# Turning routed rows on VectorE from square block loads, with up weights kept on chip, in a two-layer fp32 kernel

## The reference

```
xn = layernorm(x)
s  = attention(xn)            # two query heads, one key/value head, rope, causal softmax
g  = silu(moe(xn))            # 8 experts, top 2 of softmax(router)
x  = x + s * g
xn = layernorm(x)
s  = recurrent(xn)            # conv, decays, cumulative sums, gated feed-forward of width 512
g  = silu(tanh(xn @ w @ a1 @ a2 + bias))
out = x + s * g

moe(x) = sum over e in top2(x) of  p_e(x) * (w2_e @ (gelu(wg_e @ x + bg_e) * (w1_e @ x + b1_e)) + b2_e)
```

## Time and profile before

| | us |
|---|---|
| median of 3 runs | 563.06 |
| the three runs | 563.06, 565.64, 561.0 |
| span of the profiled execution | 567.0 |

### The profile page before, as it was taken

The page is one execution under the profiler, slowest core; times in us unless marked ns, Lnnn a source line. Parts: engine busy times, 40 slices in busy tenths (PEclk is TensorE's granted clock), DMA queues, the critical chain, the costliest instruction groups (busy, mean ns, idle before and its releaser), DMA issues. The chain is left out here.

```text
span 567.0 us, 13345 instructions
## 1 busy us (share of the span) xinstructions
PE 536.0 (95%) x3276; PEld 396.7 (70%) x3277; DVE 385.5 (68%) x1080; ACT 280.6 (50%) x797; POOL 259.1 (46%) x391
## 2 busy tenths in 40 slices
PE   9997999998989999999999999998799999999974
PEld 4745677666759999999999999964444444554441
DVE  6889777886764555555555555559588789778641
ACT  5624565645564555555555554565535644553420
POOL 4305535666502444444444444525356555664210
PEclk9998999999998999999999999999799999999998
DMA  9920553111106788878888788455000000000000
GB/s 285 392 76 33 184 195 94 61 42 61 42 14 180 235 238 233 233 233 234 237 235 237 225 241 228 134 167 144 2 0 19 18 20 0 18 18 1 19 18 18
DMA packets 46107, 71.77 MB, mean 127 GB/s; under 512 B 6256, under 2 KB 32016, under 8 KB 45824
## 3 DMA queue, kind: packets, MB, share of 16 engines
q1 hardware_dynamic: 31536, 57.82, 34.4%
q0 software_dynamic: 4320, 8.92, 4.6%
q10 hardware_dynamic: 10224, 4.73, 3.0%
HBM read 54.14 MB, written 15.74 MB: 123 GB/s over the span
## 5 line engine op out<-in xcount | busy, mean ns | idle before, releaser
L1253 DVE SCALAR_TENSOR_TENSOR AR<-bank,B1T,AR 128x128 f32<-128x128 f32 x284 | 80.0, 344 | 73.0 <-ACT AR L1667 63.1
L523 POOL DMA_INDIRECT rows_y<-YO,DST x71 | 69.8, 982 | 93.2 <-DVE YO L1237 82.5
L1667 ACT ACTIVATE AR<-bank,BGT 128x128 f32<-128x128 f32 x284 | 81.2, 368 | 60.0 <-PE bank L823 53.4
L479 POOL DMA_INDIRECT slots_x<-XR,SLOT x64 | 63.0, 984 | 50.9 <-DMA slots_x<-XR,SLOT 31.0
L823 PE MATMUL bank<-AR,WGE 128*128 128x128 f32 x568 | 75.9, 277 | 0.3 <-ACT AR L1660 0.3
L831 PE MATMUL bank<-AR,WGE 128*128 128x128 f32 x568 | 75.9, 277 | 0.0
L840 PE MATMUL bank<-W2E,AR 128*128 x568 | 75.2, 275 | 0.7 <-DVE AR L1253 0.5
L823 PEld LDWEIGHTS bank<-AR,WGE 128*128 128x128 f32 x568 | 69.8, 193 | 0.6 <-issue 0.6
L831 PEld LDWEIGHTS bank<-AR,WGE 128*128 128x128 f32 x568 | 70.0, 194 | 0.0
L840 PEld LDWEIGHTS bank<-W2E,AR 128*128 128x128 f32 x568 | 69.1, 192 | 1.1 <-issue 1.1
L1579 ACT ACTIVATE AR<-bank,AR 128x512 f32<-128x512 f32 (+1 forms) x64 | 33.8, 528 | 63.9 <-DVE AR L1173 54.5
(11 more groups left out here) (196 smaller groups left out, 944.6 us busy)
## 6 DMA issues: line engine op xcount, KB each, us to landing
WGE<-in_wgu SPq DMA_DIRECT2D x71, 512.0 KB
XG<-slots_x ACTq DMA_DIRECT2D x71, 65.0 KB
slots_x<-W1E SPq DMA_DIRECT2D x7, 585.0 KB, 10.1
X<-in_x SPq DMA_DIRECT2D x8, 256.0 KB, 5.1
W2E<-in_w SPq DMA_DIRECT2D x1, 2048.0 KB, 9.3
XR<-rows_y SPq DMA_DIRECT2D x8, 256.0 KB, 4.9
XNT<-rows_y SPq DMA_DIRECT2D x8, 256.0 KB, 5.1
out<-X SPq DMA_DIRECT2D x8, 256.0 KB, 2.3
```

The source lines that it names most:

```text
L479: pool.indirect_dma_start(out=slots_x, out_offset=bass.IndirectOffsetOnAxis(ap=SLOT[:, k, n:n + 1], axis=0), in_=XR[:, n, :], in_offset=No ...
L523: pool.indirect_dma_start(out=rows_y, out_offset=bass.IndirectOffsetOnAxis(ap=DST[q][:, 0:1], axis=0), in_=YO[q % 2][:], in_offset=None).t ...
L1253: s = dve.scalar_tensor_tensor(out=HT[u][:, c, :], in0=B[3 + u][:, c * P:(c + 1) * P], scalar=B1T[:, bass.ds(e, 1), c], in1=ZB[u][:, c, :] ...
L1667: act.activation(ZB[u][:, c, :], B[1 + u][:, c * P:(c + 1) * P], ACT.Gelu, bias=BGT[:, bass.ds(e, 1), c]).then_inc(c_gelu, 1)
```

## The change

- **Rows.** SP loads two tiles at once into XG[u] (now 128 x 256, two buffers), in four DMAs, one for each 32 features: partition 32k + r gets, for each block of 32 rows, the 32 features k of row r of that block. Each piece is 32 elements (128 bytes) long. A 128x128 tile thus lies as 16 squares of 32x32, each where its transpose belongs, and `dve.transpose`, which turns each 32x32 square by itself, writes XT. DVE turns tile j+1 ahead of the HT of tile j. PE's transposes and ACT's copies of them are gone.
- **Tags.** All tags are loaded once into TAGS by SP, in two DMAs (tiles 0 to 3, then 4 to 70), each piece two elements (8 bytes). POOL converts the destinations in two copies and waits for both before its first `c_send`. DVE reads the gate value out of TAGS.
- **Weights.** SPARE gets the up weights of all experts in one 2 MB DMA, issued by SP right after the weights of tiles 0 to 3. ACT copies the tile's 128x512 of it to WU[u], one tile ahead. Only gate weights (128x512) are loaded for each tile, and the buffer is free after the gate product.
- **SP's order.** After attention's loads SP waits for scat, loads rows of tiles 0 to 3 and the tags, then in each step loads rows (every second step) and gate weights.

```diff
-        WB = WGE[:].rearrange("p (q k) f -> p q (k f)", q=WBUFS)
+        WB = WGE[:, 0:WBUFS, :]
+        WU = WGE[:, WBUFS:WBUFS + 2, :]
-        XG = [sb(f"XG{q}", [P, ROW]) for q in range(WBUFS)]
+        XG = [sb(f"XG{u}", [P, 2 * P]) for u in range(2)]
+        r1.at = 6 * F
+        TAGS = r1.take(SLOT_TILES, 2)
+        DST = r1.take(SLOT_TILES).bitcast(U32)
+        slots_x_b = slots_x.rearrange("(n r) d -> r n d", r=BLK)
# SP
-                sp.dma_start(WB[:, q:q + 1, :], t["wgu"][:, bass.ds(e, 1), :]).then_inc(w_ld[q], 16)
+                sp.dma_start(WB[:, q:q + 1, :], t["wgu"][:, bass.ds(e, 1), 0:F]).then_inc(w_ld[q], 16)
             for j in range(WBUFS):
                 load_expert(j, j)
+            sp.dma_start(SPARE[:], t["wgu"][:, :, F:2 * F]).then_inc(ld_moe, 16)
+            def load_tiles(j, u, n):
+                for k in range(P // BLK):
+                    sp.dma_start(XG[u][k * BLK:(k + 1) * BLK, 0:n * P].rearrange("r (i c) -> r i c", c=BLK),
+                                 slots_x_b[:, bass.ds(j * (P // BLK), n * (P // BLK)), k * BLK:(k + 1) * BLK]
+                                 ).then_inc(c_ld[u], 16)
-            def c_step(j, q):
-                sp.wait_ge(c_h, j + 1)
-                load_expert(j + WBUFS, q)
+            def c_step(j, q, tiles=2, load=True):
+                if q % 2 and tiles:
+                    sp.wait_ge(c_xt, j + 1)
+                    load_tiles(j + 3, q // 2, tiles)
+                if load:
+                    sp.wait_ge(c_g, j + 1)
+                    load_expert(j + WBUFS, q)
+            sp.wait_ge(scat, 16 * 2 * NT)
+            load_tiles(0, 0, 2)
+            sp.dma_start(TAGS[:, 0:TAGS_FIRST, :], slots_x_t[:, 0:TAGS_FIRST, P:ROW]).then_inc(tags_ld, 16)
+            load_tiles(2, 1, 2)
+            sp.wait_ge(tags_ld, 16)
+            sp.dma_start(TAGS[:, TAGS_FIRST:, :], slots_x_t[:, TAGS_FIRST:, P:ROW]).then_inc(tags_ld, 16)
# POOL
-            def c_tags(j, q): ...
+            def rows_of(first, end, part):
+                pool.wait_ge(tags_ld, 16 * part)
+                pool.tensor_copy(DST[:, first:end], TAGS[:, first:end, 0]).then_inc(dst_set, 1)
+            rows_of(0, TAGS_FIRST, 1)
+            rows_of(TAGS_FIRST, SLOT_TILES, 2)
+            pool.wait_ge(dst_set, 2)
# PE
-                pe.transpose(B[7 * u][:, 0:P], XG[q][:, 0:P], ident).then_inc(c_tr, 1)
             def c_up(j, u, q):
+                pe.wait_ge(c_wu, j + 1)
-                    mm = pe.matmul(B[3 + u][:, c * P:(c + 1) * P], WB[:, q, F + c * P:F + (c + 1) * P], XT[u],
+                    mm = pe.matmul(B[3 + u][:, c * P:(c + 1) * P], WU[:, u, c * P:(c + 1) * P], XT[u],
# DVE
-                dve.wait_ge(c_tag, j + 1)
+                if isinstance(j, int) and j == 0:
+                    dve.wait_ge(tags_ld, 16)
+                if isinstance(j, int) and j == WBUFS - 1:
+                    dve.wait_ge(tags_ld, 32)
+            def c_turn(j, q):
+                dve.wait_ge(c_ld[q // 2], (j - q) * 16 + 64)
+                if not (isinstance(j, int) and j < 2):
+                    dve.wait_ge(c_h, j - 1)
+                dve.transpose(XT[q % 2], XG[q // 2][:, (q % 2) * P:(q % 2 + 1) * P]).then_inc(c_xt, 1)
# ACT
-                act.activation(XT[u], B[7 * u][:, 0:P], ACT.Copy).then_inc(c_xt, 1)
+            def c_up_weights(j, u, e):
+                if not (isinstance(j, int) and j < 2):
+                    act.wait_ge(c_h, j - 1)
+                act.activation(WU[:, u:u + 1, :], SPARE[:, bass.ds(e, 1), :], ACT.Copy).then_inc(c_wu, 1)
```

More of the change, by code:

```diff
@@ L49 @@
 WBUFS = 4
+BLK = 32
+TAGS_FIRST = 4
 SCAT_BURST = 4
@@ L302, in build @@
         o_done = sem("o_done")
-        c_ld = [sem(f"c_ld{q}") for q in range(WBUFS)]
-        c_tag = sem("c_tag")
+        c_ld = [sem(f"c_ld{u}") for u in range(2)]
+        dst_set = sem("dst_set")
         c_sum = sem("c_sum")
         w_ld = [sem(f"w_ld{q}") for q in range(WBUFS)]
-        c_tr = sem("c_tr")
+        c_wu = sem("c_wu")
+        tags_ld = sem("tags_ld")
         c_xt = sem("c_xt")
@@ L424, in _ @@
                     c_step(i * WBUFS + q, q)
-            for j in range(C_ROUNDS * WBUFS, SLOT_TILES - WBUFS):
-                c_step(j, j % WBUFS)
+            for j in range(C_ROUNDS * WBUFS, SLOT_TILES - 3):
+                c_step(j, j % WBUFS, min(2, SLOT_TILES - 3 - j), load=j + WBUFS < SLOT_TILES)
             for u in range(2):
@@ L509, in _ @@
             pool.tensor_tensor(TAPW[:, PAD - LOCAL0, :], TAPW[:, PAD - LOCAL0, :], CHN[:, 0, :], ALU.add).then_inc(w_ready, 1)
[L512 to L518, removed]
+            def rows_of(first, end, part):
+                pool.wait_ge(tags_ld, 16 * part)
+                pool.tensor_copy(DST[:, first:end], TAGS[:, first:end, 0]).then_inc(dst_set, 1)
             def c_send(j, q):
                 pool.wait_ge(c_yo, j + 1)
-                pool.wait_ge(c_tag, j + 1)
                 pool.indirect_dma_start(
-                    out=rows_y, out_offset=bass.IndirectOffsetOnAxis(ap=DST[q][:, 0:1], axis=0),
+                    out=rows_y, out_offset=bass.IndirectOffsetOnAxis(ap=DST[:, j:j + 1], axis=0),
                     in_=YO[q % 2][:], in_offset=None).then_inc(c_st[q % 2], 16)
[L527 to L533, removed]
+            rows_of(0, TAGS_FIRST, 1)
+            rows_of(TAGS_FIRST, SLOT_TILES, 2)
+            pool.wait_ge(dst_set, 2)
             for j in range(SLOT_TILES):
-                c_step(j, j % WBUFS, last=j + 2 >= SLOT_TILES)
+                c_send(j, j % WBUFS)
             pool.wait_ge(c_y, SLOT_TILES)
@@ L844, in _, with c_step @@
             e_down = pe.alloc_register("pe_expert")
-            def c_step(j, u, q, last=False):
-                if not last:
-                    c_turn(j + 1, (q + 1) % WBUFS)
+            def c_step(j, u, q):
                 c_gate(j, u, q)
@@ L861, in _ @@
             pe.wait_ge(proj_free, 4 * (NB + 1))
-            c_turn(0, 0)
             for j in range(WBUFS):
@@ L868, in _ @@
             for j in range(C_ROUNDS * WBUFS, SLOT_TILES):
-                c_step(j, j % 2, j % WBUFS, last=j == SLOT_TILES - 1)
+                c_step(j, j % 2, j % WBUFS)
             pe.reg_load(e_down, TEXP[0:1, SLOT_TILES - 1:SLOT_TILES])
@@ L1247, in c_step @@
                     dve.reg_load(e_next, TEXP[0:1, bass.ds(j + 1, 1)])
+                    c_turn(j + 1, (q + 1) % WBUFS)
                 dve.wait_ge(c_h, j + 1)
@@ L1268, in _ @@
             dve.reg_mov(e_last, e_this)
+            c_turn(0, 0)
             for j in range(WBUFS):
@@ L1670, in _, with c_step @@
             e_next, e_this = (act.alloc_register(f"act_expert_{n}") for n in ("next", "this"))
-            def c_step(j, q, last=False, load=True):
-                u = q % 2
+            def c_step(j, q, last=False):
                 e = act.snap(e_this, min_val=0, max_val=E - 1)
                 if not last:
[L1676 to L1680, removed]
                     act.reg_load(e_next, TEXP[0:1, bass.ds(j + 1, 1)])
-                c_gelu_of(j, u, e)
+                    c_up_weights(j + 1, 1 - q % 2, act.snap(e_next, min_val=0, max_val=E - 1))
+                c_gelu_of(j, q % 2, e)
                 if not last:
@@ L1697, in _ @@
             for j in range(C_ROUNDS * WBUFS, SLOT_TILES):
-                c_step(j, j % WBUFS, last=j == SLOT_TILES - 1, load=j + 3 < SLOT_TILES)
+                c_step(j, j % WBUFS, last=j == SLOT_TILES - 1)
             bring_table(ACT.Exp)
```

15 lines of the change are left out of this document (3 added, 12 removed).

## The result

| | before | after |
|---|---|---|
| median us | 563.02 (20 runs, 560.48 to 567.52) | 559.73 (20 runs, 556.73 to 562.16) |
| ratio after / before | | 0.9928, 95% interval 0.9908 to 0.9947 |
| span of the profiled execution | 567.0 | 554.9 |

What follows compares the result with a forecast made beforehand. PE, busy for all 80.00 us between 220 and 300 us, was taken as the bound. Transposes 7.6 plus stage start 0.5 gave 8.1 us: median 563.1 to 555.0, ratio 0.986; range 552 to 562.

Steps and rivals of the forecast that it cites:

- PE's transposes: 7.6 us: PE, expert stage: 69 of 71 removed transposes give 0.11 us each, 7.6 us, if PE stays the bound.
- DVE's turn costs nothing: DVE ahead of HT: a turn of 0.29 us fits into 1.05 us of idleness; uncovered it would be 21 us.
- even 0.9 us would fit: DVE's gap ahead of HT: a turn as long as 0.9 us would still be hidden in 1.05 us of idleness.
- the turn pays what it saves: Rival, chance 0.12: a wait on DVE or ACT in every tile; half of 0.11 us lost gives 559, all 563.
- over 0.8 us of gap on each: Argument against new waits on DVE and ACT: each has over 0.8 us of gap a tile.
- The stage's start: 0.5 us: Start of expert stage: first turn right behind DVE's last combine, gate at 169.0 to 169.2 instead of 169.59, gain 0.5 us.
- ACT's copy: ACT, each tile: copying up weights takes 0.62 us, fits between gelus with 0.92 us remaining, costs nothing.
- DMA: DMA engines, each tile: 1.38 us of 2.68 (51%) at 15 ns a small piece; relieved, PE stays the bound.
- the DMA rival: Row loads in every tile: small pieces make the kernel DMA-bound from 56 ns a piece, 574 at 64 ns; chance 0.08.
- The 52 ns: Row pieces of 128 bytes: cost twice a full piece, 2 x 26 ns, by the skill's rule; just under the 56 bound.
- SP's queue and tags: SP: issues take 2.0 to 3.1 of 5.36 us, hidden; 8576-piece tag load takes 8 us, lands likeliest 171 to 175.

Runs made afterwards that it cites:

- loop8_first: Changed kernel with DVE's loop of eight tiles, each turn ahead of the register load, first turn ahead of the first load; 564.97 us, ratio to before 0.9892.
- after_again: The changed kernel, unchanged, profiled and timed a second time; 568.23 us, ratio to the kernel before 0.9960.
- after_third: The changed kernel, unchanged, profiled and timed a third time; 567.78 us, ratio to the kernel before 0.9957.
- turn_twice: Changed kernel with a second DVE turn of each tile's rows into a spare buffer ahead of the real one; 576.66 us, timed once.

## Why the prediction was half right

*PE's transposes: 7.6 us.* This term was right in size. Without a transpose the gate period is 2.68 us, and with DVE relieved (loop8_first) all of it is collected: 196.3 against 188.3 us, lower clock in both, is 8.0, of which 0.4 are the one late gate of the profile before. At full clock, both worked out from their gates, it is 194.2 against 186.8, 7.4 us.

*DVE's turn costs nothing.* This step failed. The duration was nearly right: 0.29 us had been put, the fp32 turn took 312 ns. The Trainium skill (VectorE: DVE Perf Modes, The three transpose paths) gives 311 ns for a bf16 tile, and the trace agrees, for fp32.

```profile
L1252 DVE STREAM_TRANSPOSE AR<-XG 128x128 f32<-128x128 f32 x71 | 22.1, 312 | 39.4 <-PE bank L841 34.5
```

The mistake was to read DVE's 1.16 us ahead of HT as free and to write "even 0.9 us would fit". The branch and the register load stood in that gap before:

```profile
L1247 DVEq TENSOR_LOAD <-TEXP x3: 301/306/311, 280.3 to 286.0; - x3
```
```profile
L1271 DVEq COMPARE_BRANCH  x1: 56/56/56, 283.0 to 283.0; - x1
```

The tile of the earlier trace rows is the one with the branch: 0.06 us, then nothing until 0.29, then 0.21, the load from 283.59 to 283.89, and the arithmetic of waits up to 284.22, which leaves nothing free ahead of HT at 284.26, whatever releaser the row names. In the other three tiles of four the queue stood still for some 0.4 to 0.5 us there. HT could be late before by the gelus' margin without cost. The sum that was needed is this: behind L1246 (0.29 us) the load's end comes at 0.57 to 0.97 us, the turn at 0.69 to 1.17, HT 0.30 to 0.35 later; added to 1.56 us from HT to L1246 that is 2.55 to 3.07, and 10.92 for four tiles against PE's 10.72. The mean step, 2.73 us, would have fitted into the old period of 2.79; it does not fit into the new one of 2.68.

*The rival that came true* is "the turn pays what it saves": 16 x 0.21 = 3.3 us is 0.05 a tile, about half of 0.11, for which it gave 559; measured 559.7. It had a chance of 0.12, because "over 0.8 us of gap on each" was taken from busy time. Its mechanism as written, a turn of over 1.05 us, was not it.

*The stage's start: 0.5 us.* This term failed for the same reason. From the end of the combine to the gate it took 1.27 us after (162.15 to 163.42), 1.15 before. The turn did not follow the combine but the first register load, at L1283, which took 555 ns:

```profile
162.96 0.31 DVE L1252 STREAM_TRANSPOSE AR<-XG 128x128 f32<-128x128 f32 x1 [0.81 <-DVE SA L1172]
...
163.42 1.13 PE L832 MATMUL bank<-AR,WGE 128*128 128x128 f32 x8 [1.66 <-DVE AR L1252]
```

So the sum that a profile bears out is 7.6 - 3.3 - 0.1 = 4.2 us instead of 8.1. The three timed ratios of the changed kernel give 4.05 (3.0 to 5.2), 2.3 (0.8 to 3.8, after_again) and 2.5 (0.6 to 4.3, after_third). All three intervals hold 3.0 to 3.8; whether some of the 4.2, up to about 1 us, is lost outside the stage stays open. That the time fell into the forecast range is owed in part to the room that the range left for the rivals: by its mechanism the forecast was 555.

*ACT's copy.* This was right: it is hidden, took 641 ns instead of 619, and the up product never waited for it.

```profile
L1670 ACT ACTIVATE WGE<-SPARE 128x512 f32 x71 | 45.4, 641 | 2.2 <-issue 0.5
```

*DMA.* This was right in direction, with a share of 0.59 instead of 0.51. The queues from 220 to 260 us:

```profile
DMA packets 10738, 5.87 MB, mean 147 GB/s; under 512 B 8590, under 2 KB 8590, under 8 KB 10738
...
q1 hardware_dynamic: 10258, 4.89, 53.5%
q0 software_dynamic: 480, 0.98, 6.3%
```

The 7,636 pieces of 128 bytes among them took 14.7 ns on average, as the 15 from the earlier trace rows. What was under-sized is the piece of 2 KB: 84 ns in the median, but 117 on average among small ones. So the DMA rival falls. The Trainium skill (DMA: Bandwidth & Descriptors, Specifications) says that below 512 bytes the engine reads, modifies and writes; it gives no price. The 52 ns that the prediction drew from it were its own estimate, and the trace does not bear them out.

*SP's queue and tags.* This was right. Four row loads ahead of the stage take 1.84 and 1.98 us of issue and the load of 8,576 pieces 0.45, so the queue was not held. That load landed after 7.2 us (8 forecast), at about 166.4, 3 us behind the first gate (171 to 175 had been put, 2 to 6 behind it), and POOL's first send waited for DVE's result:

```profile
159.18 0.45 SPq L444 DMA_DIRECT2D W1E<-slots_x  x1
```
```profile
166.46 0.24 POOL L539 CAST W1E<-W1E 128x67 uint32<-128x67 f32 x1 [7.51 <-DMA W1E<-slots_x]
169.86 1.00 POOL L543 DMA_INDIRECT rows_y<-YO,W1E  x1 [3.15 <-DVE YO L1246]
```

## What to carry to other kernels

An idle gap of an engine is free time only after the instructions that no busy time counts are subtracted: register loads, branches, arithmetic of addresses and waits. Before work is moved to an engine, add up its whole step, instruction start to instruction start, for the worst step of the loop and for the sum over one turn of the loop, and compare it with the new, shorter period of the engine that bounds. Where a busy share says 100%, count instructions per stretch: 717 against 705 matmuls in 80 us told the period of 2.68 us from that of 2.73, and PE's busy time did not.

## What was not expected of the hardware

- A register load on DVE took 0.31 us in steady state and 0.56 us as the first one; the branch of a loop of four tiles put off what follows by 0.39 us (the load started 0.66 instead of 0.27 us after L1246). The branch itself took 0.06 us, and 0.23 us passed before the next instruction; at the last one, which leaves the loop, 0.03 us.
- A loop body of eight tiles on DVE branched at the price of one of four (0.89 us of idleness ahead of the turn), one of sixteen at 3.45 us, and PE's granted clock was half for 3.4 us behind the pause of 2.57 us.
- Two turns on DVE followed each other after 0.24 us, although the first shows 0.31 and the second 0.27 (turn_twice).
- One DMA of 8,576 pieces of 8 bytes was issued in 0.45 us and used some 10 ns of an engine for a piece (87.5% of 16 engines over 6.5 us, 9,057 packets).
